# One-core transformer layer: query and key weights loaded first in quarters, two reorderings on VectorE and ScalarE, late reads of TensorE's loop bounds

## What is computed

```python
def xattn(query, key, value, Wq, bq, Wk, bk, Wv, bv):
    q = jnp.einsum('bld,de->ble', query, Wq) + bq
    k = jnp.einsum('bld,de->ble', key, Wk) + bk
    v = jnp.einsum('bld,de->ble', value, Wv) + bv
    attn = jax.nn.softmax(jnp.einsum('bqe,bke->bqk', q, k), axis=-1)
    return jnp.einsum('bqk,bke->bqe', attn, v)

x = x + xattn(layernorm(x), ctx, ctx, Wq, bq, Wk, bk, Wv, bv)
x = x + dss(layernorm(x))          # k = Re(sum_n W exp(dt Lambda t)), y = k * u + D u, by a transform
x = x + ffn(layernorm(x))          # probs = softmax(8 gates); out = (relu(x W1[e] + b1) W2[e] + b2) * max prob
```

## Time and profile before

| | us |
|---|---|
| median of the runs (3) | 425.61 (424.99 to 425.79) |
| the profiled execution | 425.6 |
| its span, first to last instruction | 423.9 |
| TensorE busy | 393.6 (93%) |
| VectorE busy | 321.7 (76%) |
| ScalarE busy | 256.8 (61%) |
| GpSimd busy | 58.9 (14%) |
| first matmul | 11.89 |
| first softmax exponential | 42.72 |
| first expert matmul | 187.17 |

### The profile page before, as it was taken

How to read it: one execution, slowest core, us unless ns; L and a number is a source line. 1 busy time by engine, 2 the same in 40 slices (tenths; PEclk the granted TensorE clock), 3 DMA queues, 4 the chain that set the end, 5 groups by cost and what they waited for, 6 DMA issues and landing times.

```text
span 423.9 us, 5718 instructions
## 1 busy us (share of the span) xinstructions
PE 393.6 (93%) x1650; PEld 276.2 (65%) x1650; DVE 321.7 (76%) x504; ACT 256.8 (61%) x388; POOL 58.9 (14%) x59
## 2 busy tenths in 40 slices
PE   0899999999999898869999999999999999999992
PEld 0756574757985345647777677776767777676770
DVE  2688667979451686866989899898988989898880
ACT  4869687866000013057779686877968677786850
POOL 2100000000000011040040130403003040220402
PEclk9999699999999999879999999999999999999998
DMA  7996464289426940051007999979999999950100
GB/s 199 412 417 245 180 218 179 80 345 327 136 105 254 392 149 5 1 152 25 2 6 269 385 388 402 378 297 351 380 359 396 343 377 343 374 201 0 35 5 1
DMA packets 33840, 96.56 MB, mean 228 GB/s; under 512 B 2890, under 2 KB 3530, under 8 KB 32276
## 3 DMA queue, kind: packets, MB, share of 16 engines
q1 hardware_dynamic: 30324, 90.57, 58.1%
q0 software_dynamic: 1856, 5.55, 3.8%
q10 hardware_dynamic: 1632, 0.11, 0.3%
HBM read 93.04 MB, written 3.68 MB: 228 GB/s over the span
## 4 chain that ended last, share of the span: by engine, by line
PE 88%; ACT 5%; DMA 2%; DVE 2%; issue 1%; POOL 1%; SPq 0%; ACTq 0%; POOLq 0%; DVEq 0%
PE bank L1489 50%; PE bank L1313 7%; PE bank L1294 5%; PE bank L1505 4%; PE bank L1323 3%; DMA ring<-in_wq_t 2%; PE bank L1247 2%; PE bank L1359 2%; PE bank L1302 2%; PE bank L1335 2%; ACT ring L522 1%; PE bank L1366 1%; ACT ring L515 1%; PE bank L1241 1%; PE bank L1357 1%
## 5 line engine op out<-in xcount | busy, mean ns | idle before, releaser
L1138 DVE TENSOR_TENSOR w_lo<-ring,w_hi 128x1024 fp32r<-128x1024 f32 x117 | 145.3, 1268 | 25.6 <-ACT w_hi L688 24.7
L688 ACT ACTIVATE w_hi<-ring 128x1024 fp32r<-128x1024 f32 x117 | 122.1, 1053 | 48.1 <-PE bank L1489 46.9
L1489 PE MATMUL bank<-w_hi,x_hi 128*128 128x512 f32 x144 | 50.4, 431 | 3.9 <-ACT w_hi L688 3.9
L1489 PE MATMUL bank<-ring,work 128*128 128x512 f32 x108 | 49.3, 592 | 0.0
L1489 PE MATMUL bank<-w_hi,x_lo 128*128 128x512 f32 x144 | 46.2, 402 | 0.0
L1489 PE MATMUL bank<-w_lo,x_hi 128*128 128x512 f32 x144 | 46.2, 402 | 0.0
L1489 PEld LDWEIGHTS bank<-w_hi,x_hi 128*128 128x128 f32 x144 | 27.1, 194 | 13.2 <-ACT w_hi L688 6.3
L1489 PE MATMUL bank<-w_hi,h_hi 128*128 128x512 f32 x90 | 33.3, 452 | 0.0
L1221 POOL TENSOR_TENSOR small<-small,x_ext 128x512 f32<-128x512 f32 x9 | 14.8, 1639 | 131.4 <-ACT small L696 131.4
L1489 PEld LDWEIGHTS bank<-w_lo,x_hi 128*128 128x128 f32 x144 | 27.6, 192 | 6.7
L1489 PEld LDWEIGHTS bank<-w_hi,x_lo 128*128 128x128 f32 x144 | 27.6, 192 | 6.7
(11 more groups left out here) (189 smaller groups left out, 615.6 us busy)
## 6 DMA issues: line engine op xcount, KB each, us to landing
ring<-in_w SPq DMA_DIRECT2D x32, 2048.0 KB, 11.3
ring<-in_ctx_turned SPq DMA_DIRECT2D x4, 2048.0 KB, 12.8
ring<-in_ctx SPq DMA_DIRECT2D x4, 2048.0 KB, 14.7
x_ext<-sorted_rows POOLq DMA_DIRECT2D x9, 257.0 KB, 3.2
work<-in_b SPq DMA_DIRECT2D x8, 256.0 KB, 8.1
ring<-in_wq_t SPq DMA_DIRECT2D x1, 1024.0 KB, 10.1
x_ext<-in_x SPq DMA_DIRECT2D x1, 1024.0 KB, 12.5
tab<-in_tables SPq DMA_DIRECT2D x1, 627.5 KB, 13.3
```

The source lines that it names most:

```text
L688: act.activation(w_hi[:, n % NSPLIT, :, :], weight_part(e, n), ACT.Identity).then_inc(hi_ready, 1)
L1138: dve.tensor_tensor(w_lo[:, n % NSPLIT, :, :], weight_part(e, n), w_hi[:, n % NSPLIT, :, :], ALU.subtract).then_inc(lo_ready, 1)
L1489: ins = pe.matmul(dst, kept, moved, start=start and g == 0 and q == 0, stop=stop and g == 1 and q == len(terms) - 1)
```

## The change

- `log_dt` goes from the head of SyncE's DMA queue to the head of ScalarE's. SyncE now issues the key weights first, then the query weights in four DMAs of 128 input rows (256 KB) with a semaphore each, then x and the rest.
- The key weights get three columns of zeros (260 instead of 257), and the products are 258 columns wide.
- TensorE's fold runs with the quarter `e` as the outer loop: four matmuls, one for each bank, per quarter, accumulating in four banks at once. The bias products come behind all of them.
- VectorE normalizes x and copies tiles 0 and 2 ahead of roundings 1 and 2.
- ScalarE makes 7 turns, then copies the folded weights, makes 4 turns, copies tiles 1 and 3, and makes the last 4.
- In the gate stage `time_normalized(3)` stands ahead of `rows_low(2)`.
- TensorE reads its first bound ahead of the expert loop and each further one at the head of its expert.

```diff
+WK = DC + 4
-        wk_at = 4 * D - DCH * (DC + 1)
+        wk_at = 4 * D - DCH * WK
@@ sync
-            sp.dma_start(dt_sb, log_dt.partition_broadcast(P)).then_inc(params_loaded, 16)
             sp.dma_start(wk_sb, wkb_t.rearrange("(e p) c -> p e c", p=P)).then_inc(qk_loaded, 16)
-            sp.dma_start(wq_sb, wq_t.rearrange("(e p) d -> p e d", p=P)).then_inc(qk_loaded, 16)
+            for e in range(DCH):
+                sp.dma_start(wq_sb[:, e, :], wq_t[e * P:(e + 1) * P, :]).then_inc(wq_loaded[e], 16)
@@ scalar
+            act.dma_start(dt_sb, log_dt.partition_broadcast(P)).then_inc(params_loaded, 16)
...
-            turns(1, AH)
+            turns(1, AH // 2)
             for d in range(DCH):
                 weights_copy(d)
+            turns(AH // 2, AH - 4)
             turned_rows(1)
             turned_rows(3)
+            turns(AH - 4, AH)
             a_sines(0)
@@ vector
             a_phases(0)
-            a_phases(1)
...
-            a_phases(2)
             normalized(which, range(NB), [xn1[:, b, :] for b in range(NB)], xn1_ready)
...
+            a_phases(1)
+            a_phases(2)
             a_phases(3)
...
+            time_normalized(3, which)
             rows_low(2)
-            time_normalized(3, which)
@@ tensor
-            pe.wait_ge(qk_loaded, 32)
-            for d in range(DCH):
-                dst = may_fill(pe, ("wqk", d))
+            pe.wait_ge(qk_loaded, 16)
+            for e in range(DCH):
+                pe.wait_ge(wq_loaded[e], 16)
+                for d in range(DCH):
+                    dst = may_fill(pe, ("wqk", d)) if e == 0 else bank[:, S_BANK[d], :]
+                    ins = pe.matmul(dst[:, 0:DC + 2], wq_sb[:, e, col_slice(d)], wk_sb[:, e, 0:DC + 2],
+                                    start=e == 0, stop=e == DCH - 1)
+                    if e == DCH - 1 and d < DCH - 1:
+                        did_fill(ins, ("wqk", d))
...
-            bounds = [pe.value_load(win_i[0:1, e:e + 1], min_val=0, max_val=MAXW) for e in range(NE + 1)]
+            bounds = [pe.value_load(win_i[0:1, 0:1], min_val=0, max_val=MAXW)]
             for b in range(8):
                 pe.wait_ge(drained[b], FILL_COUNT[b])
             for e in range(NE):
+                bounds.append(pe.value_load(win_i[0:1, e + 1:e + 2], min_val=0, max_val=MAXW))
                 with pe.If(bounds[e] < bounds[e + 1]):
```

More of the change, by code:

```diff
@@ L289, in perceiver_layer @@
         bkq_loaded = sem("bkq_loaded")
+        wq_loaded = [sem(f"wq{e}_loaded") for e in range(DCH)]
         qk_loaded, bv_loaded, wri_loaded = sem("qk_loaded"), sem("bv_loaded"), sem("wri_loaded")
@@ L1241, in keep_warm @@
                     pe.matmul(bank[:, O_BANK, 0:row.shape[1]], row[:, 0:P], row, start=True, stop=True)
-            pe.wait_ge(qk_loaded, 32)
-            for d in range(DCH):
-                dst = may_fill(pe, ("wqk", d))
-                for e in range(DCH):
-                    ins = pe.matmul(dst[:, 0:DC + 1], wq_sb[:, e, col_slice(d)], wk_sb[:, e, :],
-                                    start=e == 0, stop=e == DCH - 1)
-                if d == DCH - 1:
-                    pe.wait_ge(bkq_loaded, 16)
-                    for c in range(CCH):
-                        for e in range(DCH):
-                            pe.matmul(dst[:, DC + 4 + c:DC + 5 + c], wk_sb[:, e, col_slice(c)], bkq_sb[:, e, 1:2],
-                                      start=e == 0, stop=e == DCH - 1)
-                    pe.wait_ge(tab_loaded, 16)
-                    pe.wait_ge(bkq_ready, 1)
-                    ins = pe.matmul(dst[:, DC + 6:DC + 7], ones, bkq_sum, start=True, stop=True)
-                did_fill(ins, ("wqk", d))
+            pe.wait_ge(qk_loaded, 16)
[7 more added lines that the diff above has]
+                        did_fill(ins, ("wqk", d))
+            pe.wait_ge(bkq_loaded, 16)
+            for c in range(CCH):
+                for e in range(DCH):
+                    pe.matmul(dst[:, DC + 4 + c:DC + 5 + c], wk_sb[:, e, col_slice(c)], bkq_sb[:, e, 1:2],
+                              start=e == 0, stop=e == DCH - 1)
+            pe.wait_ge(tab_loaded, 16)
+            pe.wait_ge(bkq_ready, 1)
+            did_fill(pe.matmul(dst[:, DC + 6:DC + 7], ones, bkq_sum, start=True, stop=True), ("wqk", DCH - 1))
             for b in range(NB):
@@ L1593 @@
         "wq_t": g["L0_xattn_Wq"].T,
-        "wkb_t": np.concatenate([g["L0_xattn_Wk"].T, g["L0_xattn_bk"][:, None]], 1),
+        "wkb_t": np.concatenate([g["L0_xattn_Wk"].T, g["L0_xattn_bk"][:, None], np.zeros((D, WK - DC - 1), np.float32)], 1),
         "bkq": np.stack([g["L0_xattn_bk"], g["L0_xattn_bq"]], 1),
```

## The result

The changed kernel took 428.27 us (median of 17 runs, 425.66 to 430.8), the kernel before 425.44 us (17 runs on the same chip): ratio 1.0057, 95% interval 1.0035 to 1.0078. The forecast was 424.2 us with a range of 422.0 to 426.4; both the sign and the range missed.

What follows compares the result with a forecast made beforehand. TensorE was taken to bound nearly everything from the first softmax on, after a relay between engines at the start. Forecast: 425.6 - 1.7 (late bounds reads) + 0.3 (start) + 0 (gate) = 424.2 us, range 422.0 to 426.4.

Steps and rivals of the forecast that it cites:

- part 3: Expert entry: TensorE reads its bounds late, so the first expert matmul starts sooner; gain taken as 1.7 us.
- parts 1, 2 and 4: Start and gate: weights first in quarters, new VectorE and ScalarE orders, gate order; +0.3 us from the start, gate 0.
- The loads in the loop cost 0: Expert loop: seven bounds loads moved into it are covered by the sequencer's lead; cost 0, without the cover 5.8 us.
- Rival 4: Expert loop: the bounds loads there are not hidden and add 5.8 us, giving 429.7 us; chance 0.03.
- The first quarter lands at 7.4 us: Start: first quarter of the query weights lands at 7.4 us (7.0 to 8.2), so the fold ends near 16.3, not 20.8.
- ScalarE loses nothing by log_dt's place: Start: log_dt on ScalarE's queue delays lam and times perhaps 0.8 us; first seven turns end near 13.3, needed at 16.4.
- The query product starts 1.2 to 2.0 us sooner: Start: transposes follow the normalized tiles sooner, so the query product, before at 25.38 us, starts 1.2 to 2.0 us sooner.
- part 2: Start: VectorE normalizes earlier and ScalarE's turns are reordered; with the earlier weight loads it sums to +0.3 us.
- Softmax at 42.5 to 43.2: ScalarE's first softmax, before at 42.72 us, was forecast to start at 42.5 to 43.2 us.
- The term 18.1 + 5.7 us: ScalarE from fourth weight copy to softmax: 18.1 us of earlier work plus eight turns, 5.7 us.
- the third rival: Start: TensorE idles, the clock falls, query and score products pay about 1.7 us each; 428.1 us, chance 0.07.
- Part 4: 0: Gate stage: one normalization ahead of one subtraction gains 0 to 0.1 us, taken as 0.

Runs made afterwards that it cites:

- late_bounds_only: Kernel before with only the late bounds reads (one ahead of the experts, one at each expert's head): 428.21 us, ratio 1.005.
- times_first: Changed kernel with lam and times issued ahead of log_dt on ScalarE's queue: 428.05 us, ratio 1.004.
- bounds_first_again: Changed kernel with all nine bounds read ahead of the experts again: 426.01 us, ratio 1.0001.
- quarters_dt_first: Kernel before with query weights in quarters and the fold with e outside, log_dt still first on SyncE's queue: 425.35 us, ratio 0.9979.
- loads_only: Kernel before with log_dt on ScalarE's queue, query weights in quarters and the fold with e outside; orders and bounds as before: 428.47 us, ratio 1.0051.
- late_pad80_split: Kernel before with late bounds reads and 80 semaphore increments on TensorE, 66 at the head and 14 behind the fold's matmuls: 424.41 us, ratio 0.9943.

## Why the prediction was wrong, step by step

The sum was 425.6 - 1.7 + 0.3. The step that turned the sign is the term put at nothing, the loads in the expert loop: at the border over expert 1 the profiled execution lost 3.1 us. By the runs the other parts came out near the sum (part 3 without the stall -1.7 to -2.0, parts 1, 2 and 4 together 0.0), but the way to the 0.0 was not the one forecast: later work at the start and a lower level that fell elsewhere cancelled, which is luck.

- **The loads in the loop cost 0.** Wrong in effect. The loads themselves are hidden at every border, as the 4.4 us of lead said. But with them in the loop, most executions stall at the border over expert 1: 2.8 us of TensorE waiting in the profiled one, 5 to 6 us between the two levels of execution times (424.1 and 429.9). Rival 4 had a chance of 0.03 and another mechanism. Since TensorE idles there, the clock can fall too: in late_bounds_only it is 0.50 from 241.2 to 244.5 us.
- **The first quarter lands at 7.4 us.** Wrong. The first product began at 9.65 and the fold took 10.15 us instead of 8.9; it ended 1.0 us sooner, not 4. I let the first quarter pass as if it alone used the DMA engines. With log_dt issued two places later (times_first) the fold began at 6.78. What the Trainium skill says against this (DMA: Bandwidth & Descriptors, "Issuing engines are not separate DMA queues"), that DMAs issued by different engines run on the same 16 DMA engines, I had weighed for x only; the trace agrees, since log_dt on the other queue delayed the weights. "TensorE does not starve" held: the list has one wait for the query weights, 9.7 us, and none between quarters. The longer fold is slow products: from 13.2 to 14.9 us the trace has 5 of them, in bounds_first_again, where the fold took 8.60 us, it has 9. The granted clock is shown as 1.00 in both; the cause is open.
- **"ScalarE loses nothing by log_dt's place."** The delay was far larger than the 0.8 us that I allowed, and times_first and quarters_dt_first show whose it is: the turns start 3.9 us later, seven of them end at 16.4 instead of 13.3. In the changed kernel it did not bind all the same, for ScalarE then waited 2.1 us for the fold. In loads_only, where fifteen turns stand ahead of the copies, it did.
- **The query product starts 1.2 to 2.0 us sooner.** Wrong: 0.9 later. The transposes were 1.0 sooner as told (21.57), yet the product also needs the row copies of ScalarE, which part 2 had put behind four turns. I had counted these turns for the softmax and not for TensorE.
- **Softmax at 42.5 to 43.2.** It was 45.11. The term 18.1 + 5.7 us was right: from the fourth weight copy at 21.74 it gives 45.5. What failed is where it starts, 18.7 to 19.4, and that comes from the fold, which ended near 19.8 us, with the bias products and the last product behind it; VectorE's bias sum, which I had put last, was ready at 18.68. VectorE's query copy was at 34.98, late for TensorE's sake (1.08 us of waiting) and not for the roundings'.
- **The clock.** The condition that I named for being wrong, a low clock in 21 to 38 us, came true (25.9 to 29.2 us, at half of 2.4 GHz) right behind TensorE's wait of 2.8 us for the row copies; the product took 8.59 us instead of 7.10. This is the third rival's mechanism, at one place instead of two, and near 46 us it gave back. My word "lull" for the low stretch at 42.6 us does not fit its row: TensorE was busy for 3.40 of the 3.40 us before it, with 1-column products among them.
- **Part 3's gain of 1.7 us.** Right for the entry: 3.20 - 1.55 = 1.65 us in the changed kernel, by the sequencer's earlier arrival. In late_pad80_split the entry gains only 1.0 us (from the last bank copy's end at 184.68 to 186.87), and the first 24 products take 7.40 us instead of 8.40, with less of the lower level; the sum comes to the forecast by two terms instead of one.
- **Part 4: 0.** Right as far as seen: from the first values product to the gate's last transposes the chain takes 112.45 us in both traces (56.46 to 168.91, and 55.27 to 167.72). No run has it alone.

## What to carry to other kernels

Before work is moved behind a wait, see who used that wait: the eight turns had lain in ScalarE's idle time and afterwards stood in the only chain to the softmax, which no earlier start of TensorE could shorten. Here a branch over a large block of straight code was followed by a wait that no other engine explains, and edits far ahead of it (fewer reads, 24, 48 or 80 increments) changed how often it came. So look for waits on issue right behind a taken branch and for the instruction packets in the list of DMA queues, and take several executions, since one profile shows only one level. Test a change of several parts part by part: here a part worth about 2 us in one kernel and three that cost nothing together added up to a loss.

## What the runs showed of the hardware

- Code came in packets of 16 KB, 13 in a run on the queue that I take for TensorE's. In executions with one packet less during expert 0 the sequencer stood still for 5.3 to 6.5 us at the border, and TensorE waited 2.2 to 3.8 us.
- The two levels appear between executions of the same kernel (24 increments: 7 at 423.9 to 425.1 us, 5 at 429.7 to 430.6). The kernel before also has some at 428.5 to 430.7 us (4 of 29 and 6 of 23 measured together), of which there is no profile.
- A semaphore increment on TensorE's sequencer is not free: 80 at the head took 12.2 us, 0.15 us each.
- Two parts that cost 0.5% and 0.9% alone cost 0.0% together. In the traces the softmax comes at 45.33, 45.64 and 44.38 us, the first values product at 56.68, 58.16 and 54.04: 11.4, 12.5 and 9.7 us between them, and only the third has no stretch at the lower level there.
